# First feed-forward layer of an attention block: six chunks transposed by DMA, the GELU scale in a register, weight codes made a stage earlier, b2 added beside layer two, 23 paired range units

## What is computed

```
x = x + xattn(layernorm(x), ctx)              # 32 turns, one per item
y = layernorm(x)
def qlinear(x, W, b):
    xq, sx, zx = affine_quantize(x)           # needs min and max over ALL of x
    wq, sw = sym_quantize(W)
    return (xq - zx) @ wq.T * (sx * sw) + b
h = gelu(qlinear(y, W1, b1))                  # 3200 x 1024
x = x + qlinear(h, W2, b2)                    # 3200 x 256
```

## Time and profile before

| | us |
|---|---|
| median of 3 runs (1048.63 to 1048.99) | 1048.63 |
| the profiled execution: first to last instruction (its span) | 1046.4 |
| attention turns up to the last one's first half | to about 958 |
| last turn's end, range of y, first codes | 958 to 972.2 |
| layer one | 972.2 to 1016.9 |
| range of h, layer two, output | 1016.9 to 1046.4 |

### The profile page before, as it was taken

The page is one execution under the profiler, slowest core; times in us unless marked ns, Lnnn a source line. Parts: engine busy times, 40 slices in busy tenths (PEclk is TensorE's granted clock), DMA queues, the critical chain, the costliest instruction groups (busy, mean ns, idle before and its releaser), DMA issues.

```text
span 1046.4 us, 38342 instructions
## 1 busy us (share of the span) xinstructions
PE 1017.4 (97%) x10877; PEld 653.0 (62%) x10877; DVE 918.9 (88%) x2748; ACT 868.2 (83%) x1828; POOL 786.3 (75%) x1118
## 2 busy tenths in 40 slices
PE   8999999999999999999999999999999999998858
PEld 6664666666666666666666666666666666666327
DVE  7877888888889888888888888888898988886998
ACT  5755888888888888888888888888888888885976
POOL 3356888888888888888888888888888888884880
PEclk9999999999999999999999999999999999999989
DMA  8502676767766677776776766667667666663303
GB/s 246 147 1 55 132 142 137 141 138 143 145 137 138 138 144 145 145 142 137 142 141 137 142 132 142 138 139 141 137 138 143 137 140 139 138 141 77 119 0 127
DMA packets 436830, 137.12 MB, mean 131 GB/s; under 512 B 409058, under 2 KB 435782, under 8 KB 436806
## 3 DMA queue, kind: packets, MB, share of 16 engines
q1 hardware_dynamic: 436806, 136.82, 63.0%
HBM read 28.60 MB, written 6.55 MB: 34 GB/s over the span
## 4 chain that ended last, share of the span: by engine, by line
PE 92%; DVE 5%; issue 1%; ACT 1%; POOL 0%; DVEq 0%; ACTq 0%; POOLq 0%
PE front L384 18%; PE front L386 17%; PE front L385 17%; PE back L1503 14%; PE front L1481 7%; PE tp L1481 6%; PE front L1449 2%; PE front L1450 2%; PE front L1455 2%; DVE hrange L1256 1%; PE front L1620 1%; DVE hrange L1257 1%; PE back L384 1%; PE back L386 1%; PE back L385 1%
## 5 line engine op out<-in xcount | busy, mean ns | idle before, releaser
L635 POOL TENSOR_TENSOR hl<-prob,hl 100x361 f16<-100x361 f32 x511 | 431.4, 853 | 123.7 <-ACT hl L808 75.0
L802 ACT ACTIVATE prob<-prob,nmax 100x361 f32<-100x361 f32 x512 | 291.0, 587 | 8.0 <-DVE nmax L1068 8.0
L1503 PEld LDWEIGHTS back<-v,pT 128*128 128x128 f16 (+1 forms) x4608 | 174.2, 97 | 49.9 <-issue 9.6
L1503 PE MATMUL back<-v,pT 128*128 128x65 f16 (+1 forms) x4608 | 188.3, 193 | 0.0
L808 ACT ACTIVATE hl<-prob 100x361 f16<-100x361 f32 x352 | 176.0, 500 | 4.5
L812 ACT ACTIVATE k_h<-front 128x362 f16<-128x362 f32 x256 | 119.8, 468 | 63.1 <-PE front L386 60.1
L1135 DVE SCALAR_TENSOR_TENSOR k_l<-front,k_h 128x362 f16<-128x362 f32 x256 | 136.4, 533 | 22.6 <-ACT k_h L812 19.5
L1068 DVE CUSTOM_DVE_ANT_0 prob<-tp,mask_g,ngain 100x361 f32<-100x361 f32 x256 | 150.2, 587 | 0.6 <-POOL hl L635 0.6
L1068 DVE CUSTOM_DVE_ANT_0 prob<-front,mask_g,ngain 100x361 f32<-100x361 f32 x256 | 148.4, 589 | 2.5 <-PE front L1481 1.6
L384 PE MATMUL front<-wv_h,ctx_h 128*128 128x512 f16 (+1 forms) x384 | 147.2, 383 | 1.2 <-DVE k_l L1135 1.1
L386 PE MATMUL front<-wv_h,ctx_l 128*128 128x512 f16 (+1 forms) x384 | 145.5, 379 | 0.0
(11 more groups left out here) (236 smaller groups left out, 2116.2 us busy)
## 6 DMA issues: line engine op xcount, KB each, us to landing
ctx_raw<-ctxT SPq DMA_DIRECT2D x33, 361.0 KB, 3.1
pT<-hl SPq DMA_TRANSPOSE x254, 3.5
xs<-x SPq DMA_DIRECT2D x8, 400.0 KB
q_all<-x SPq DMA_DIRECT2D x32, 100.0 KB
out<-q_all SPq DMA_DIRECT2D x32, 100.0 KB
xb<-out SPq DMA_DIRECT2D x5, 640.0 KB, 8.3
out<-xb SPq DMA_DIRECT2D x25, 128.0 KB, 1.8
q_all<-wq SPq DMA_DIRECT2D x2, 512.0 KB, 5.5
```

The source lines that it names most:

```text
L635: pool.tensor_tensor(hl[0:T, n % RT, 1, 0:S], prob[0:T, n % RP, 0:S], hl[0:T, n % RT, 0, 0:S], ALU.subtract).then_inc(s_lo, 1)
L802: act.activation(prob[0:T, n % RP, 0:S], prob[0:T, n % RP, 0:S], ACT.Exp, bias=nmax[0:T, n:n + 1], scale=-1.0).then_inc(s_exp, 1)
L1503: ins = pe.matmul(obank[j % 2][:, n % GH * DV:(n % GH + 1) * DV], pT[0:r, n % RT, part_ * ST + st, :], v2[half][0:r, st, v, n % HT, :], st ...
```

## The change

- `yT` gets the layout item, half of the features, 112 token columns. Chunks 0 and 1 go through PE and DVE as before. The codes of chunks 2 to 7 are written to the attention's buffer `hl`, and SP transposes each chunk with one DMA (128 partitions x 8 x 112) when its codes are ready. ACT's six copies, the "Y" jobs and `FJOBS` are gone. SP issues the six transposes ahead of the five loads of the residual.
- ACT loads the GELU scale once into a register (`reg_load`), and the GELUs take it from there; the bias is still read from SBUF.
- `w_codes(2)` and `w_codes(3)` move to POOL's last turn, between the last `AL` and `POW`.
- `PAIRED` has 23 units instead of 17, `LAG` is 6 instead of 5, and POOL makes all differences first and then all ten pieces of b2, each pair after its own load. DVE waits for the piece that a block needs, block by block.

```
-PAIRED = (3, 5, 8, 10, 12, 14, 18, 19, 20, 21, 23, 24, 26, 27, 29, 30, 31)
-LAG = 5
-FJOBS = [job for g in range(NU) for job in ([("Y", g // NF + 1)] if g % NF == 2 and g < NU - NF else []) + [("G", g)]]
+PAIRED = (4, 5, 7, 8, 9, 10, 11, 13, 14, 15, 16, 18, 19, 20, 21, 23, 24, 25, 26, 28, 29, 30, 31)
+LAG = 6
...
-    y16 = place("y16", [P, B, D], F16)
-    yT = place("yT", [P, KD, B * T], F16)
+    y16 = place("y16", [P, 2 * TB, D], F16)
+    y16_dma = hl[:, :, :, :].rearrange("p r w s -> p (r w s)").rearrange("p (b d) -> p b d", d=D)
+    yT = place("yT", [P, B, KD, TR], F16)
...
+        for c in range(2, NB):
+            sp.wait_ge(*y_ready(c))
+            sp.dma_start_transpose(yT[:, c * TB:(c + 1) * TB, :, :], y16_rows(c, TR)).then_inc(s_yd2[c - 2], 16)
         sp.wait_ge(s_xo, 16 * B)
...
-        differences(0, 1)
-        w_codes(2)
-        differences(1, 3)
-        w_codes(3)
...
+        differences(0, len(PAIRED))
         pool.wait_ge(s_b12, 48)
...
+        for n in range(2 * NX):
+            if n % 2 == 0:
+                pool.wait_ge(s_xi[n // 2], 16)
+            add_b2(n, n + 1)
...
+        s1 = act.alloc_register("s1")
+        act.reg_load(s1, sc[0:1, S1:S1 + 1].bitcast(I32))
+        for g in range(NU):
+            act.wait_ge(s_f1, g + 1)
             pair, m = divmod(g, NF)
-            act.activation(hid[:, 2 * pair:2 * pair + 2, m, :], wide[j % 3][:, :, 0:TW], ACT.Gelu,
-                           bias=b1c[:, m:m + 1], scale=sc[:, S1:S1 + 1]).then_inc(s_ge, 1)
+            act.activation(hid[:, 2 * pair:2 * pair + 2, m, :], wide[g % 3][:, :, 0:TW], ACT.Gelu,
+                           bias=b1c[:, m:m + 1], scale=s1).then_inc(s_ge, 1)
...
         def outputs(c):
             for n in blocks_of(c):
+                dve.wait_ge(s_xb, n // RB * 2 + (1 if n % RB < 3 else 2))
                 dve.wait_ge(s_f2, n + 1)
...
-        dve.wait_ge(s_xb, 2 * NX)
...
+                ins = pe.matmul(wide[g % 3][:, n, 0:TW].rearrange("p (i t) -> p i t", i=TB), w1q[:, k, m * P:(m + 1) * P],
+                                yT[:, c * TB:(c + 1) * TB, k, 0:T], start=k == 0, stop=k == KD - 1)
```

## The result

The changed kernel is slower: a median of 1053.42 us (1052.04 to 1054.53, 5 runs) against 1048.93 (1048.63 to 1049.11, 5 runs) for the kernel before, a ratio of 1.0047 with a 95% interval of 1.0034 to 1.006. The forecast was 1044.6, its range 1043.8 to 1048.8. The profiled execution took 1052.72 us, its span is 1049.9. Of all the executions used in this document one, of the kernel before beside e9, was in a slower state (1073.24 us), and its ratio leaves it out.

What follows compares the result with a forecast made beforehand. DVE was taken to bound layer one, never waiting there. Ranges -4.8, waits for ACT +0.5 and register load +0.3 gave -4.0 us, span 1042.4; with 2.2 added, 1044.6 us, range 1043.8 to 1048.8.

Steps and rivals of the forecast that it cites:

- The ranges, their rates, and what ACT makes of them: Layer one: 23 paired units cut DVE's range work by 4.8 us; DVE waiting for ACT gives back 0.5.
- The sum: Whole kernel: -4.8 for ranges, +0.5 for DVE waiting for ACT, +0.3 for the register load, -4.0 us in all.
- the register load: ACT, between last code of y and first GELU: taken to cost 0.3 us, bounds nothing and 0.8.
- The register: ACT in layer one: a GELU with its scale in a register falls from 0.90 to 0.815 us.
- rival 3: Layer one: the register saves nothing, GELU stays at 0.90, stage ends 2.5 us later, total 1047.1 us; chance 0.10.
- Transposes: y's chunks by DMA: land 2.9 us after issue, before PE needs them; cost nothing, up to about 1 us if late.
- PE's split reads: Layer one matmuls reading four runs of 100 columns: taken to cost nothing; at half rate, some 9 us longer.
- codes of W2: POOL's last turn: 4.4 us hidden in its idle time; taken at nothing, 0.3 as bound if DAL is held.
- the choice in layer two: POOL's b2 additions beside DVE's codes of h: taken as DVE keeping its lengths, no cost; forecast's chance 0.42.
- rival 1: Layer two: DVE instructions wait for the end of POOL additions under way, 3.5 us, total 1048.1 us; chance 0.32.
- Rival 2: Layer two: POOL keeps its turn until all ten additions are done, DVE starts 6.1 us later, 1054.7 us; chance 0.07.

Runs made afterwards that it cites:

- e9: Changed kernel with its ten b2 additions replaced by one POOL addition per attention turn, placed in the next turn; 1044.10 us, 0.9971 of the kernel before.
- e7: Changed kernel without the b2 additions, with the 17 paired units and lag of the kernel before; 1048.29 us, 0.9998 of the kernel before.
- e1: Changed kernel with the ten b2 additions on POOL left out, loads and waits kept; 1044.63 us, 0.9968 of the kernel before.
- e6: Changed kernel without the b2 additions and with the GELU scale read from SBUF instead of a register; 1046.24 us.
- e2: Changed kernel with each b2 addition replaced by a POOL memset of about the same length, which reads nothing; 1051.52 us, one run.
- e3: Kernel before with only its ten b2 additions moved behind the last difference and block-by-block waits; 1055.35 us, 1.0066 of the kernel before.
- e5: Changed kernel with its ten b2 additions cut into 25 of one block each; 1048.01 us, one run.

## Why the prediction was wrong

**The ranges, their rates, and what ACT makes of them: right.** The sum had -4.0 for the stage (-4.8 + 0.5 + 0.3), measured -4.19: -4.74 for the ranges, +0.72 for DVE waiting for ACT, and -0.17 where the register load had +0.3. The six units alone gave -4.00 (e7 against e1), so one unit is worth 0.67 net of DVE's waits.

**The register: right.** 0.815 forecast, 0.81 measured; rival 3's 2.5 for its absence, 2.44 measured (e6). The load was given 0.3 and cost nothing.

**Transposes, PE's split reads, codes of W2: right.** 3.1 us to landing; PE waits for ACT's GELUs in layer one (10.7 us of its weight loads' waits), not for DMA; the matmuls of a unit, which now read four runs of 100 columns, start 0.17 us apart (976.20, 976.37, 976.54) as those of 400 columns in one run did (975.76, 975.93, 976.10); `DAL` was held as the step's bound said, and the sum behind it came 0.15 later, within the 0.3 allowed, where the forecast took nothing.

**The step that failed is the choice in layer two.** The prediction named the mechanism and priced it as rival 1, at 3.5 us and a chance of 0.32, and took "DVE keeps its length" for the forecast. Two things were wrong in it.

*The row it decided by.* It chose by DVE's L947 at 43.35, which kept its 1.28 us beside a POOL instruction of 1.02 that was there first. Those two columns of 4 values are not like 768 values read twice, as the step itself said; why that one didn't hold DVE, no run shows. The opposite row, POOL's 1.23 instead of 0.19, was the one to go by: it showed that the two engines do exclude each other. But its L947 has two inputs in SBUF, like the product L1291; a conversion or a clamp has one, so it is no row for them. The trace of the kernel before had such a row, beside the clamps of the earlier trace rows (971.37 to 972.37), and it was overlooked:

```profile
971.59 1.68 POOL L686 TENSOR_SCALAR y<-y,sc 100x1024 f16<-100x1024 int16 x1
...
974.47 1.19 POOL L686 TENSOR_SCALAR y<-y,sc 100x1024 f16<-100x1024 int16 x1
```

Beside DVE's clamps POOL's code took 1.68 us instead of 1.19. There too DVE was first. e2, e3 and `DAL`'s 1.39 show the case that no row before had, a long POOL instruction that is under way, or starts in the same instant.

*The price, had rival 1 been taken.* It let a new addition in only when DVE was doing something else, so two before the first output, 1.0 each, and 1.5 behind it. In fact one addition gets in between any two DVE instructions of the kinds concerned, even when the second stands ready: seven waits before the first output, 0.59 to 1.61 each, 7.4 in all. And it left out what the starved PE does next: its clock fell to the lower level, 1.8 us more in this profile. 3.5 should have been 9.2, and rival 1 would have given 1053.8, beside the 1053.4 measured.

**Rival 2** put 6.1 on one instruction, and its total of 1054.7 is near; but its mechanism is not what happened: the first conversion was held for 0.59, not until the additions ended.

**Left open.** Why PE's granted clock is low at 953 us in some profiles of the same turns and not in others, about 1 us of difference, isn't settled; no run was made for it. Nor is it settled how much of the 1.8 us behind the first output another execution would show.

## What to carry to other kernels

Before work is moved to POOL, list what DVE runs in that stretch. Beside reductions and instructions that have one of their two inputs in PSUM it was free here; beside conversions and clamps from SBUF to SBUF, and products of two SBUF tiles if POOL reads, each DVE instruction waits for the rest of one POOL instruction. If it can't be avoided, cut POOL's work into short instructions, and put it where another engine, not DVE, sets the pace. A step that is put into a full turn belongs behind the point where its input is long ready: a wait is paid by all that is queued behind it.

## What the runs showed of the hardware

- DVE and POOL, both with work ready, took turns one instruction at a time: 7 DVE instructions were held by 7 additions in 12.1 us (changed kernel, 1013.26 to 1025.32). At 971.37 in the kernel before two clamps of DVE, 0.54 us each, ran back to back although POOL's L686 had been issued 0.23 before the second, so the turns aren't strict everywhere. POOL's additions are stretched too, ten took 16.84 us instead of 5 x 3.04 = 15.2.
- A tiny instruction with two inputs in SBUF is held like a large one: a product of 128x1 values took 1.77 us instead of 0.16 beside an addition, 0.68 beside short ones (e5), 0.14 beside a memset (e2). Instructions of one column with one input kept their 0.15 to 0.20.
- An ACT instruction of 128x800 from PSUM to SBUF took 1098 ns with its scale in SBUF, 939 with it in a register.
- PE, starved of codes in the changed kernel (busy for 2.66 of the 6 us from 1018), went from the granted clock of 1.00 to 0.50 and issued 16 matmuls in 3 us there, 30 at 1.00.
